# Twelve transposes of the identity ahead of TensorE's projection of the second half of the heads' values

## The reference

```python
def _L3_gnn_ref(x, adj, Wq, Wk, Wv, Wo):
    q = heads(x @ Wq)
    k = heads(x @ Wk)
    v = heads(x @ Wv)
    scores = jnp.einsum('bhnd,bhmd->bhnm', q, k) / sqrt_dk
    scores = jnp.where(mask, scores, -jnp.inf)
    attn = jax.nn.softmax(scores, axis=-1)
    out = jnp.einsum('bhnm,bhmd->bhnd', attn, v)
    return jax.nn.relu(out) @ Wo
```

## Time and profile before

| | |
|---|---|
| Timed runs (3) | median 3795.36 us, 3793.58 to 3798.09 |
| Profiled execution | 3815.43 us, span 3813.8 us, mean granted clock 0.961 |
| TensorE busy | 3324.7 us (87%) in 18048 matmul instructions |
| Weight loads busy | 2558.3 us (67%) |
| DVE busy | 2460.1 us (65%) |
| ACT busy | 2204.2 us (58%) |
| GpSimd busy | 773.0 us (20%) |
| DMA | 40.24 MB, mean 11 GB/s |

### The profile page before, as it was taken

The page is one execution under the profiler, slowest core; times in us unless marked ns, Lnnn a source line. Parts: engine busy times, 40 slices in busy tenths (PEclk is TensorE's granted clock), DMA queues, the critical chain, the costliest instruction groups (busy, mean ns, idle before and its releaser), DMA issues.

```text
span 3813.8 us, 59841 instructions
## 1 busy us (share of the span) xinstructions
PE 3324.7 (87%) x18048; PEld 2558.3 (67%) x18048; DVE 2460.1 (65%) x7151; ACT 2204.2 (58%) x4349; POOL 773.0 (20%) x1052
## 2 busy tenths in 40 slices
PE   6689989898898899889998898989989898899866
PEld 4576766767667676666766677676766766667653
DVE  3466676666757666676666767666676666767654
ACT  3256556665565756656665575756656665565623
POOL 1212122121211222121121212122121121211210
PEclk8899999999999999999999999999999999999988
DMA  5000000000000000000000000000000000000000
GB/s 137 1 1 12 7 12 7 7 7 7 12 7 10 3 7 12 7 12 7 7 7 7 12 7 12 1 7 12 7 12 7 7 6 7 12 7 1 1 6 6
DMA packets 39858, 40.24 MB, mean 11 GB/s; under 512 B 7264, under 2 KB 38240, under 8 KB 39520
## 3 DMA queue, kind: packets, MB, share of 16 engines
q1 hardware_dynamic: 31072, 27.68, 2.4%
q0 software_dynamic: 8448, 8.39, 1.5%
HBM read 36.07 MB, written 8.39 MB: 12 GB/s over the span
## 4 chain that ended last, share of the span: by engine, by line
PE 48%; issue 25%; ACT 11%; DVE 11%; POOL 4%; DVEq 0%; DMA 0%; POOLq 0%; ACTq 0%; SPq 0%
PE acc L1187 11%; PE work L1209 9%; PE acc L1223 7%; PE acc L1289 3%; PE work L1130 3%; ACT PT L1036 3%; PE acc L1258 3%; POOL rstd L510 2%; PE acc L1270 2%; PE acc L1318 2%; PE work L1103 2%; PE work L1238 2%; ACT L1036 2%; PE work L1173 1%; DVE stats L759 1%
## 5 line engine op out<-in xcount | busy, mean ns | idle before, releaser
L1209 PE MATMUL work<-XT,w_sb 128*128 128x256 f32 x3072 | 732.7, 384 | 36.7 <-DVE XT L816 15.0
L510 POOL TENSOR_TENSOR rstd<-var_eps,minus_half 128x2 f32<-128x2 f32 x320 | 225.1, 703 | 2641.4 <-DVE var_eps L768 2641.2
L1223 PE MATMUL acc<-w_sb,gT 128*128 128x256 f32 x3072 | 731.4, 385 | 0.0
L1209 PEld LDWEIGHTS work<-XT,w_sb 128*128 128x128 f32 x3072 | 557.6, 190 | 168.2 <-ACT gT L1018 35.5
L1223 PEld LDWEIGHTS acc<-w_sb,gT 128*128 128x128 f32 x3072 | 579.9, 193 | 97.8 <-issue 22.8
L1018 ACT ACTIVATE gT<-work,b_sb 128x256 f32<-128x256 f32 x768 | 343.1, 473 | 208.6 <-PE work L1209 201.1
L1187 PE MATMUL acc<-X,PT 128*128 128x256 f32 x1536 | 387.6, 410 | 24.8 <-ACT PT L986 24.2
L1187 PEld LDWEIGHTS acc<-X,PT 128*128 128x128 f32 x1536 | 312.7, 207 | 108.8 <-issue 46.3
L1018 ACT ACT_TABLE_LOAD x198 | 254.0, 1283 | 3.5
L752 DVE COPY PT<-work 128x512 f32<-128x512 f32 x160 | 109.5, 684 | 225.5 <-PE work L1173 223.8
L759 DVE BATCH_NORM_STATS2 stats<-R 128x6 f32<-128x256 f32 x640 | 240.9, 418 | 11.0
(11 more groups left out here) (153 smaller groups left out, 5934.7 us busy)
## 6 DMA issues: line engine op xcount, KB each, us to landing
HX<-in_x SPq DMA_DIRECT2D x16, 512.0 KB, 3.8
pos<-in_adj POOLq DMA_DIRECT2D x16, 512.0 KB, 5.7
out<-X SPq DMA_DIRECT2D x32, 256.0 KB, 2.1
w_sb<-in_L_gnn_W SPq DMA_DIRECT2D x6, 1024.0 KB, 8.4
g_sb<-in_L_gnn_g SPq DMA_DIRECT2D x6, 128.0 KB, 6.7
awr_sb<-in_L_gnn_attn_w SPq DMA_DIRECT2D x2, 256.0 KB, 7.9
c_sb<-in_L_gnn_beta SPq DMA_DIRECT2D x3, 128.0 KB, 4.5
PT<-in_L_gnn_b SPq DMA_DIRECT2D x3, 128.0 KB, 5.7
```

The lines of the kernel that those rows point to most:

```text
L510: pool.tensor_tensor(rstd[s][:, half_rows(half)], var_eps[s][:, half_rows(half)], minus_half[:], ALU.pow)\
L1209: last = pe.matmul(u.bank[:, 0:HN], w1_sb[:, l, c, f * P:(f + 1) * P], XT[s][:, c, half * HN:(half + 1) * HN], start=(c == 0), stop=(c == ...
L1223: last = pe.matmul(acc[s][half][:, i, :], gT[s][:, f, i * P:(i + 1) * P], w2_sb[:, l, f, :], start=(f == 0 and i == 0), stop=(f == FC - 1) ...
```

## The change

A table FILLERS names stages and numbers of transposes. It has one entry, 12 for v1 of L3. A new function fill_in multiplies the identity by the identity so many times into the first 128 columns of a bank; fill_in_ahead first waits for the bank of the use it is given. Nothing reads what the fill writes: the stage's own product starts anew in the same bank. All other calls find no entry in the table and emit nothing. In weights_transposed the wait for the bank is moved ahead of the wait for the exp.

```diff
--- before.py
+++ after.py
@@ -138,6 +138,10 @@
         ("middle", "L1.2", "sum0 norm0 agg1"), ("starting", "L0", "v0"),
     ]
 
+
+
+    FILLERS = {("L3", "v1"): 12}
+
     def half_batch(middle, other, after, ending=True, starting=True):
         place = {"middle": (middle, 0), "ending": (other, after), "starting": (other, after + 1)}
         left_out = ([] if ending else ["ending"]) + ([] if starting else ["starting"])
@@ -1095,6 +1099,16 @@
                 pe.wait_ge(loaded[key], 16 * N_LOADS[key])
                 pe.wait_ge(folded[key], N_FOLDED[key])
 
+            def fill_in(bank, stage, key):
+                for _ in range(FILLERS.get((key, stage), 0)):
+                    pe.transpose(bank[:, 0:P], ident[:], ident[:])
+
+            def fill_in_ahead(s, it, use, stage, key):
+                if (key, stage) in FILLERS:
+                    u = Use(s, it, use, 0)
+                    pe.wait_ge(u.evacuated, u.turn)
+                    fill_in(u.bank, stage, key)
+
             def transpose_tiles(s, it, key, src, row_tiles):
                 for c in range(DC):
                     u = Use(s, it, key, c)
@@ -1109,6 +1123,7 @@
                         pe.wait_ge(x_in.sems[s], x_in.value(it, "L0", 15))
                         transpose_tiles(s, it, "xT L0", HX[s], range(NT))
                     else:
+                        fill_in_ahead(s, it, f"xT{half} {key}", f"xT{half}", key)
                         pe.wait_ge(normed.sems[s], normed.value(it, MADE_BY[key], half))
                         transpose_tiles(s, it, f"xT{half} {key}", X1[s], tiles(half))
                 return stage
@@ -1122,6 +1137,7 @@
                 def stage(s, it, key):
                     weights, columns = {"L0": (w0_sb, DA), "L2": (wg_sb, DA), "L3": (wv_sb, D)}[key]
                     if key != "L0" or half == 0:
+                        fill_in_ahead(s, it, "v L0" if key == "L0" else f"v{half} {key}", f"v{half}", key)
                         wait_transposed(s, it, key, half)
                     for t in tiles(half):
                         u = Use(s, it, "v L0", t) if key == "L0" else Use(s, it, f"v{half} {key}", t % HT)
@@ -1163,12 +1179,13 @@
 
             def weights_transposed(t):
                 def stage(s, it, key):
+                    u = Use(s, it, f"pT {key}", t)
+                    pe.wait_ge(u.evacuated, u.turn)
+                    fill_in(u.bank, f"pT{t}", key)
                     if key == "L2":
                         pe.wait_ge(kept.sems[s], kept.value(it, key, t))
                     else:
                         pe.wait_ge(exp_done.sems[s], exp_done.value(it, key, t))
-                    u = Use(s, it, f"pT {key}", t)
-                    pe.wait_ge(u.evacuated, u.turn)
                     for j in range(NT):
                         last = pe.transpose(u.bank[:, j * P:(j + 1) * P], T[s][:, t, j * P:(j + 1) * P], ident[:])
                     last.then_inc(u.filled, 1)
@@ -1177,6 +1194,7 @@
             def agg(half):
                 def stage(s, it, key):
                     pe.wait_ge(acc_evacuated[half].sems[s], acc_evacuated[half].value(it, key) - 1)
+                    fill_in(flat(acc[s][half]), f"agg{half}", key)
                     src = SOURCE[key] if key in L1K else V
                     if key in L1K[1:] and half == 0:
                         pe.wait_ge(affine_done.sems[s], affine_done.value(it, L1K[L1K.index(key) - 1] + " x", 1))
@@ -1191,6 +1209,7 @@
 
             def h_transposed(half):
                 def stage(s, it, key):
+                    fill_in_ahead(s, it, f"hT{half} {key}", f"hT{half}", key)
                     pe.wait_ge(normed.sems[s], normed.value(it, key + " h", half))
                     transpose_tiles(s, it, f"hT{half} {key}", HX[s], tiles(half))
                 return stage
@@ -1199,6 +1218,7 @@
                 def stage(s, it, key):
                     l = L1K.index(key)
                     if quarter == 0:
+                        fill_in_ahead(s, it, f"g{half} {key}", f"f1{half}0", key)
                         for c in range(DC):
                             u = Use(s, it, f"hT{half} {key}", c)
                             pe.wait_ge(u.evacuated, u.turn + 1)
```

## The result

The changed kernel takes 3781.9 us in the median of 5 runs (3774.9 to 3786.8), the kernel before 3795.4 (5 runs, 3786.8 to 3798.1). An execution over 1.5% longer than the fastest of its kernel is a slow one and left out of every comparison; there was one, of the kernel before, with 4033.9 us. The ratio is 0.9969, with a 95% interval of 0.9956 to 0.9983: faster by 0.3%, where 0.7% were forecast. The two profiled executions are 3815.4 and 3784.0 us, 31.4 apart.

The account below looks back on a forecast made before the run. TensorE, busy 87% of the span, sets the time by its pace and pauses. Terms: -25 (ten long stretches) - 3.8 (three short) + 2 (last call) = -26.8 us, -0.70%, giving 3769 us from the 3795.4 median; range 3750 to 3801.

Parts of the forecast that it names:

- The fill stands behind the idling: Ahead of v1 of L3, 1.42 us of idling stay and twelve transposes push v1 back by 1.3 us.
- The cover: DVE's queue hides the fill in 15 calls, with 1.2 us to spare for the sums and 1.3 for copying k.
- The clock stays up: Behind v1, less idling before sq1 keeps the clock at 1.00 in nearly all 15 calls; agg0 takes 3.55 us.
- The other edits: Swapped waits ahead of the weights' transposes, empty fills and two more waits per v1 call: all at zero.
- The closing call: Last v1 call, with no other batch to cover the fill: costs 1.3 to 2.6 us, taken as 2.
- the last of the sum: Final step: -26.8 us on the profiled 3815.4 is -0.70%, applied to the median 3795.4 for 3769 us.
- ten long and three short slow stretches: Low clock behind v1: ten calls at 0.76 gain 2.5 us each, 25; three at 0.88 gain 1.25 each, 3.8.
- a rival with 0.13 for both halves: Behind v1, the clock falls as before, or timed runs never had these slow stretches: 3797 us; chance 0.13.
- the local rows: From v1's start to the first L1270, 16.60 us against 13.52: a slow stretch costs 3.08 us.
- Later slow stretches take some back: Slow stretches later in the half batch move with the work and take part of the gain back; 2.5 us taken.
- The rival of the long half batches: Later slow stretches change places: fourteen long half batches, not five, give 3800 us, none 3750; chance 0.15 for shifting four or more.

Follow-up runs that it names:

- f1: Changed kernel with 24 transposes ahead of v1 instead of 12; ratio 0.9984 to the kernel before, median 3794.0 us.
- f5: Changed kernel with no fill ahead of v1 and the 12 transposes in the pause before sq1; ratio 0.9967 to the kernel before, median 3787.7 us.
- e3: Changed kernel with the 12 transposes replaced by three full-array float32 identity products of 256 columns; ratio 0.9955 to the kernel before.
- e2: Changed kernel with the 12 transposes replaced by two products using 4 of 128 rows, taking the same time; ratio 1.0004 to the kernel before.
- e1: Changed kernel with FILLERS empty, leaving only the new order of the two waits; ratio 0.9989 to the kernel before.
- e0: Kernel before, unchanged, run and profiled again; ratio 1.0022 to the kernel before, profiled execution 3795.1 us.
- h0: Kernel before, unchanged, one more execution with its trace; profiled execution 3792.4 us.
- h1: Kernel before, unchanged, profiled once more; profiled execution 3798.4 us.
- f4: Changed kernel plus 12 transposes behind rb1 and 8 each ahead of the normed-row waits in xT0 and xT1 of L1.0 and L2; ratio 0.9952 to the kernel before.

## Why the prediction was half right

- The fill stands behind the idling, lasts 1.3 us, and is covered by DVE: right. In eleven of the fifteen calls the wait is 1.42 us, sq1 stands at 8.90 (forecast 8.89), agg0 at 9.97 (9.97), and the pause is 1.33 (1.35). ACT's first exp slipped by 0.6 us (5.08 behind the wait, before 4.47), not 0.3, and was absorbed all the same.
- The cover is finite: right, but it is better than read. Of the 1.3 us beyond it, 0.3 to 0.4 reach sq1 and agg0 (f1).
- The clock stays up: right, in 15 calls of 15, in three profiled executions. That filling the pause of 1.70 us is enough is shown by f5; that transposes count, by e3; that a fill of 4 rows only moves the fall, by e2.
- The other edits cost nothing: right within 0.2% (e1).
- The closing call costs 2 us: it cost 1.3. The fill took 2.5 us at the low clock, the work behind it ran faster, and sq1 came 9.24 behind the wait, before 7.96. The lines of the changed kernel:

```profile
3701.41 2.73 PE L1104 MATMUL work<-ident 128*128 128x128 f32 x12 [2.12 <-DVE head_min L871]
3703.94 2.40 PE L1146 MATMUL work<-wv_sb,XT 128*128 128x256 f32 x8
...
3710.65 0.70 PE L1278 MATMUL acc<-X,R 32*128 32x512 f32 x2 [0.88 <-DVE X L858]
```

- The step that failed is the last of the sum: "-26.8 on 3815.4 is -0.70%; on the median it gives 3768.7". It carried ten long and three short slow stretches from one profiled execution to executions that have others, and the count is the mis-sized term. By the forecast's own prices, 2.5 and 1.25 us each and 2 us for the last call, e0 (two long, nine short) gives 14 us, h0 (five and four) 15.5, h1 (four and five) 14: about 0.4%, and measured were 0.31, 0.47 and 0.48%. Read at proj0, these executions lose 20 to 22 us in the slow stretches and the first profile 36.6. That the profiled execution lay 0.5% above the median was in the text, as half of a rival with 0.13 for both halves ("never had these slow stretches"). The truth lies between that rival and the forecast.
- For the profiled pair the sum came near, 26.8 us forecast and 31.4 measured, but partly by luck. The price of a long stretch was taken as 2.5, between 3.08 and 2.0, and the 2.0 compares unlike half batches: of its three, only the one from 1927.3 holds a turn of the loop. Without a turn it is 228.7 against 225.7, which is 3.0, as in the local rows. The short ones were taken at 1.25; in e0 proj0 is late by 1.6 (87.8 and not 86.2). So, less what the change still loses there and the 1.3 us of the last call, some 35 us were to be won up to proj0 in the pair, and 18 to 20 against e0, h0 and h1.
- "Later slow stretches take some back" was allowed for within the 2.5, and they did. At proj0 the low clock was 51 to 55 us in four executions of before and 61 to 65 in three of the changed kernel (0.91 and 0.83 above). Over the whole span, outside the stretches behind v1, it was 203 to 231 us in the four and 245 to 255 in the three: of the 44 to 79 us of low clock that the fill removed, some 30 turned up elsewhere. How much time this costs was not measured by itself.
- The rival of the long half batches counted the turn of the loop as a slow stretch: the five long ones in the earlier trace rows's kernel (230.8 to 232.3 us) all hold a turn, so fourteen of them were never possible. What is left of the rival stays open as to its size; after the change the half batches with a turn last 227.5 to 230.5 us, those without 225.5 to 226.5.

## What to carry to other kernels

When TensorE's clock falls at a pause, filling the pause with matmuls or transposes of the full array whose result nobody reads can pay (0.3 to 0.5% here), if another engine's queue covers what they push back. Price it by the stretch, then count the stretches in several executions before multiplying: a profiled time above the range of the timed runs says that its pattern isn't the typical one. Compare stretches that hold the same work, turns of a loop included. And put the fill where TensorE idles: in f4, where it didn't, the higher clock bought nothing that the fill hadn't spent.

## What the runs showed of the hardware

- One kernel on one chip (34 executions of the kernel before): executions from 3782.9 to 3820.7 us, 1%, with mean granted clocks of 0.959 to 0.970. The four longest (3808.5 to 3820.7) have 0.959 to 0.961, the three shortest (3782.9 to 3784.1) 0.968 to 0.970.
- A product that uses 4 of 128 rows keeps TensorE busy in the profile and did not hold the clock: 0.52 right behind it (e2). Twelve transposes of 128 rows in its place held it in every such call.
- TensorE's branch at the end of a round of the loop took 3.3 to 3.7 us where it went back (six times) and 0.08 where it didn't, and TensorE idled for its last 1.6 to 2.1 us; the same branch took 0.04 to 0.07 us on the other engines.
